# A window-attention block: the wide half of its second MLP matrix in three rounded passes

## The reference

```python
xn = layernorm(x, ln1_w, ln1_b)
xw = windows(jnp.roll(xn, (-3, -3), (1, 2)))          # (-1, 49, 192)
q, k, v = heads(xw @ qkv_w + qkv_b)
o = softmax(q @ k.T * 32 ** -0.5) @ v
x = x + unroll(o @ proj_w + proj_b)
h = layernorm(x, ln2_w, ln2_b)
h = gelu(h @ mlp_w1 + mlp_b1)                         # exact gelu, 768 wide
x = x + (h @ mlp_w2 + mlp_b2)
```

## Time and profile before

| | before |
|---|---|
| median of 3 runs | 3153.24 us (3152.94 to 3154.19) |
| profiled execution | 3154.41 us, its span 3152.6 us |
| TensorE matmuls | 3103.1 us, 98% of the span |
| TensorE weight loads | 2689.8 us, 85% |
| VectorE | 2200.5 us, 70% |
| ScalarE | 1971.1 us, 63% |
| GpSimd | 696.8 us, 22% |
| mean granted TensorE clock | 0.995 of full |

### The profile page before, as it was taken

How to read it: one execution, slowest core, us unless ns; L and a number is a source line. 1 busy time by engine, 2 the same in 40 slices (tenths; PEclk the granted TensorE clock), 3 DMA queues, 4 the chain that set the end, 5 groups by cost and what they waited for, 6 DMA issues and landing times.

```text
span 3152.6 us, 112135 instructions
## 1 busy us (share of the span) xinstructions
PE 3103.1 (98%) x44212; PEld 2689.8 (85%) x44212; DVE 2200.5 (70%) x5902; ACT 1971.1 (63%) x3595; POOL 696.8 (22%) x782
## 2 busy tenths in 40 slices
PE   6999999999999999999999999999999999999998
PEld 5888888888888888888888888888888888888887
DVE  4677777677776776677767777767776777767774
ACT  3666666666666666666666666666666666666664
POOL 1222222222222222222222222222222222222220
PEclk8999999999999999999999999999999999999999
DMA  1001001000100010001001000100010001001100
GB/s 45 25 26 28 23 23 28 26 23 23 29 25 23 25 28 23 23 26 28 23 23 27 26 23 23 29 25 23 23 29 24 23 25 28 23 23 26 27 23 17
DMA packets 112145, 79.77 MB, mean 25 GB/s; under 512 B 10129, under 2 KB 111603, under 8 KB 112115
## 3 DMA queue, kind: packets, MB, share of 16 engines
q1 hardware_dynamic: 112114, 79.35, 9.6%
HBM read 40.78 MB, written 38.54 MB: 25 GB/s over the span
## 4 chain that ended last, share of the span: by engine, by line
PE 97%; issue 1%; POOL 0%; DVE 0%; ACT 0%; DMA 0%; SPq 0%; POOLq 0%; DVEq 0%; ACTq 0%
PE ps L741 34%; PE ps L808 17%; PE ps L744 15%; PE ps L817 9%; PE ps L778 5%; PE ps L840 5%; PE ps L860 4%; PE ps L704 3%; PE ps L712 2%; PE ps L825 2%; PE ps L828 1%; PE ps L714 1%; DMA xin<-in_x 0%; POOL xb L355 0%; DVE st L391 0%
## 5 line engine op out<-in xcount | busy, mean ns | idle before, releaser
L741 PE MATMUL ps<-zh,w 128*128 128x392 f32 x3072 | 708.6, 345 | 0.6 <-ACT zh L586 0.6
L808 PE MATMUL ps<-g,w 128*128 128x392 f32 x1536 | 586.2, 504 | 0.0
L741 PEld LDWEIGHTS ps<-zh,w 128*128 128x128 f32 x3072 | 537.2, 189 | 22.3 <-ACT zh L586 0.9
L741 PE MATMUL ps<-zh,wqkv 128*128 128x400 f32 x1536 | 418.9, 381 | 0.0
L808 PEld LDWEIGHTS ps<-g,w 128*128 128x128 f32 x1536 | 261.2, 190 | 143.7 <-issue 36.5
L664 ACT ACTIVATE g<-ps,biasf 128x392 f32<-128x392 f32 x768 | 372.7, 563 | 3.3 <-PE ps L741 3.3
L363 POOL TENSOR_TENSOR ve<-mv,eps 98x4 f32<-98x4 f32 x256 | 50.9, 199 | 1402.2 <-DVE mv L396 1402.2
L391 DVE BATCH_NORM_STATS2 st<-xin 98x6 f32<-98x192 f32 x512 | 145.8, 348 | 302.8 <-DMA xin<-in_x 302.8
L629 ACT ACTIVATE yT<-ps,b 128x392 f32<-128x392 f32 x128 | 75.1, 587 | 422.5 <-PE ps L808 422.5
L404 DVE TENSOR_SCALAR z<-x,mv,rs 98x192 f32<-98x192 f32 (+2 forms) x768 | 208.5, 345 | 186.7 <-POOL rs L365 186.7
L741 PEld LDWEIGHTS ps<-zh,wqkv 128*128 128x128 f32 x1536 | 290.9, 190 | 41.6
(11 more groups left out here) (92 smaller groups left out, 5779.1 us busy)
## 6 DMA issues: line engine op xcount, KB each, us to landing
xin<-in_x SPq DMA_DIRECT2D x128, 147.0 KB
out<-yo SPq DMA_DIRECT2D x128, 147.0 KB
xin<-in_x SPq DMA_DIRECT2D x128, 71.2 KB
out<-yo SPq DMA_DIRECT2D x128, 71.2 KB
xin<-in_x SPq DMA_DIRECT2D x128, 54.8 KB
out<-yo SPq DMA_DIRECT2D x128, 54.8 KB
xin<-in_x SPq DMA_DIRECT2D x128, 18.8 KB
out<-yo SPq DMA_DIRECT2D x128, 18.8 KB
```

The source lines that it names most:

```text
L741: last = pe.matmul(dst, cols(w, part), act_ if zh is zh2 else windows(act_, WIDE, EVEN), start=(n == 0), stop=(n == 4))
L808: last = pe.matmul(ps[:, Y[0], 0:M], w2[:, k, 0:A], g[:, k, :], start=(k == 0), stop=(k == KC - 1))
```

## The change

The wide half of the second MLP matrix is computed in three rounded passes for each of its six chunks. The weight gets a high part `w2h` and a low part `w2l` once at the start. Of g, the high part `gh` is a copy that rounds, made for chunks 0 to 2 by ScalarE (`high_gelu`) and for 3 to 5 by GpSimd; the low part `gl` = g - gh is made by GpSimd for all six (`gelu_parts`), after its half of the normalisation and ahead of the two rstd computations. The narrow half stays float32. ScalarE does Gelus 0 to 3, roundings 0 and 1, the two copies of probabilities, rounding 2, Gelus 4 and 5. TensorE turns the probabilities before it transposes z1; the wide half stands as chunks 0 and 1 before pv, 2 and 3 after the narrow half, 4 and 5 after the projection, in each pair the low parts of g last. The banks move: q to 7, the result Y to 4 and 5, the probabilities to 4 then 2, the projection to 2 and 3. With them the waits move: pv waits for both copies, the projection for both low parts of its input before it starts, `turn_result` for the residual. TensorE waits for `projb_ready` before the first scores, as the bias product lies in bank 3. The copy of qA is in two parts (214 and 186 columns), and the second half of the scores of heads 0 to 3 waits for the second.

```diff
+        w2h = sb("w2h", [128, KC, A], F32R)
+        w2l = sb("w2l", [128, KC, A], F32R)
...
+        gh = sb("gh", [128, KC, M], F32R)
+        gl = sb("gl", [128, KC, M], F32R)
...
-        QK = (0, 1, 6)
+        QK = (7, 1, 6)
...
-        Y = (7, 6)
+        Y = (4, 5)
...
-        TP = (2, 4)
+        TP = (4, 2)
         PV = 2
-        PROJ = (4, 5)
+        PROJ = (2, 3)
         OFFSETS = (4, 7)
-        PROJ_OFFSET = 7
+        PROJ_OFFSET = 3
+        Q_CUT = 4 * EVEN + WIDE - EVEN
...
+        ACT_HIGH = 3
...
+            def gelu_parts(prev):
+
+                wait(pool, y_done, 2, prev - 1, 2)
+                for m in range(KC):
+                    if m < ACT_HIGH:
+                        wait(pool, gh_act, ACT_HIGH, prev, m + 1)
+                    else:
+                        wait(pool, g_done, KC, prev, m + 1)
+                        pool.nop(nofuse=True)
+                        pool.tensor_copy(gh[:, m, :], g[:, m, :]).then_inc(gh_pool, 1)
+                        wait(pool, gh_pool, KC - ACT_HIGH, prev, m + 1 - ACT_HIGH)
+                    pool.tensor_tensor(gl[:, m, :], g[:, m, :], gh[:, m, :].bitcast(F32), ALU.subtract)\
+                        .then_inc(gl_done, 1)
+
...
                     normalise(pool, i, 0)
+                if feeds(i):
+                    gelu_parts(i - 1)
+                if attends(i):
                     if more(i + 1):
                         rstd(mv1, ve1, rs1, mv1_done, ve1_done, rs1_done, i + 2, z1_done)
...
+                low_weight(W2, [(w2l[:, :, :], w2[:, :, 0:A], w2h[:, :, :], None)])
...
-                act.activation(qA[:, 0:N], ps[:, QK[0], 0:N], ACT.Identity, bias=biasf[:, Q0:Q0 + 1])\
-                   .then_inc(qk_ready, 1)
+                for cols in (slice(0, Q_CUT), slice(Q_CUT, N)):
+                    act.activation(qA[:, cols], ps[:, QK[0], cols], ACT.Identity, bias=biasf[:, Q0:Q0 + 1])\
+                       .then_inc(qk_ready, 1)
...
+            def high_gelu(prev, m):
+
+                wait(act, g_done, KC, prev, m + 1)
+                act.activation(gh[:, m, :], g[:, m, :], ACT.Copy).then_inc(gh_act, 1)
+
...
+                high_weight(W2, [(w2h[:, :, :], w2[:, :, 0:A], 1.0)])
...
-                    for m in range(KC):
-                        wait(act, h_done, KC, prev, m + 1)
-                        act.activation(g[:, m, :], ps[:, H[m], 0:M], ACT.Gelu, bias=biasf[:, HID0 + m:HID0 + m + 1])\
-                           .then_inc(g_done, 1)
+                    for m in range(4):
+                        gelu(prev, m)
+                    high_gelu(prev, 0)
+                    high_gelu(prev, 1)
...
+                if feeds(i):
+                    high_gelu(prev, 2)
+                    gelu(prev, 4)
+                    gelu(prev, 5)
                 if more(i):
                     wait(act, v_done, 1, i, 1)
                     high_parts1(i + 1)
...
-                wait(pe, qk_ready, 2, i, 2)
-                wait(pe, x2_done, 2, i - 1, 2)
+                wait(pe, qk_ready, 3, i, 2)
+                wait(pe, yT_ready, 2, i - 2, 2)
                 for q, k, heads, row, col in ((qA, kA, (0, 1, 2, 3), 0, 0), (qB, kB, (4, 5), 64, PAIRS * TOK)):
                     for half in range(2):
+                        if half == 1 and q is qA:
+                            wait(pe, qk_ready, 3, i, 3)
...
+                dst = ps[:, Y[0], 0:M]
+                if 0 in chunks and attends(prev + 1):
+                    wait(pe, pt_ready, 2, prev + 1, 1)
                 for k in chunks:
-                    wait(pe, g_done, KC, prev, max(k + 1, H.index(Y[0]) + 1))
-                    last = pe.matmul(ps[:, Y[0], 0:M], w2[:, k, 0:A], g[:, k, :], start=(k == 0), stop=(k == KC - 1))
+                    if k < ACT_HIGH:
+                        wait(pe, gh_act, ACT_HIGH, prev, k + 1)
+                    else:
+                        wait(pe, gh_pool, KC - ACT_HIGH, prev, k + 1 - ACT_HIGH)
+                    pe.matmul(dst, w2h[:, k, :], gh[:, k, :], start=(k == 0), stop=False)
+                    pe.matmul(dst, w2l[:, k, :], gh[:, k, :], start=False, stop=False)
+                for k in chunks:
+                    wait(pe, gl_done, KC, prev, k + 1)
+                    last = pe.matmul(dst, w2h[:, k, :], gl[:, k, :], start=False, stop=(k == KC - 1))
...
+                if attends(prev + 1):
+                    wait(pe, x2_done, 2, prev + 1, 2)
...
-                    if feeds(i) and half == 0:
-                        wait(pe, g_done, KC, i - 1, 4)
+                    if feeds(i):
+                        wait(pe, g_done, KC, i - 1, 2 * half + 2)
...
+                wait(pe, pt_ready, 2, i, 2)
+                pe.nop(nofuse=True)
                 for half in range(2):
-                    wait(pe, pt_ready, 2, i, half + 1)
-                    pe.nop(nofuse=True)
...
-                wait(pe, oh_ready, 2, i, 1)
+                wait(pe, ol_ready, 2, i, 2)
                 for p in range(BLOCKS):
-                    waits = {} if p else {2: [(ol_ready, 2, i, 1)], 3: [(ol_ready, 2, i, 2)]}
...
             pe.wait_ge(pads_ready, 2)
+            pe.wait_ge(projb_ready, 1)
...
+                if attends(i):
+                    turn_probs(i)
                 if more(i):
                     wait(pe, z1_done, 1, i + 1, 1)
                     wait(pe, s_sub, 2, i, 2)
                     transposes1()
-                if attends(i):
-                    turn_probs(i)
-                if feeds(i):
-                    mlp2_wide(prev, range(0, 3))
+                if feeds(i):
+                    mlp2_wide(prev, (0, 1))
                 if attends(i):
                     pv(i)
                 if feeds(i):
                     mlp2_narrow(prev)
-                    mlp2_wide(prev, range(3, 4))
+                    mlp2_wide(prev, (2, 3))
                 if attends(i):
                     proj(i)
                 if feeds(i):
-                    mlp2_wide(prev, range(4, KC))
+                    mlp2_wide(prev, (4, 5))
```

More of the change, by code:

```diff
@@ L164, in swin_kernel @@
         g_done = sem("g_done")
+        gh_act = sem("gh_act")
+        gh_pool = sem("gh_pool")
+        gl_done = sem("gl_done")
         y_done = sem("y_done")
@@ L613, in values, with gelu @@
                                ACT.Copy).then_inc(v_ready, 1)
+            def gelu(prev, m):
+                wait(act, h_done, KC, prev, m + 1)
+                act.activation(g[:, m, :], ps[:, H[m], 0:M], ACT.Gelu, bias=biasf[:, HID0 + m:HID0 + m + 1])\
+                   .then_inc(g_done, 1)
+            def high_gelu(prev, m):
+                wait(act, g_done, KC, prev, m + 1)
+                act.activation(gh[:, m, :], g[:, m, :], ACT.Copy).then_inc(gh_act, 1)
             def exponential(i, part, slots):
@@ L750, in qk @@
                 wait(pe, zl1_done, 2, i, 2)
-                if tiles == (2,):
-                    wait(pe, yT_ready, 2, i - 2, 1)
                 for t in tiles:
@@ L867, in proj @@
                     pe.wait_ge(w_lo, PROJ_W + 1)
-                wait(pe, oh_ready, 2, i, 1)
+                wait(pe, ol_ready, 2, i, 2)
                 for p in range(BLOCKS):
-                    waits = {} if p else {2: [(ol_ready, 2, i, 1)], 3: [(ol_ready, 2, i, 2)]}
                     last = project(ps[0:PART, PROJ[p // 2], 256 * (p % 2):256 * (p % 2) + C], oh, ol, wproj,
-                                   lambda w, part: w[:, part, :], tokens=span(p), waits=waits)
+                                   lambda w, part: w[:, part, :], tokens=span(p))
                     if p % 2:
@@ L904, in body @@
                         pe.wait_ge(weight_loaded[W2], 16 * LOADS[W2])
-                        pe.wait_ge(w_lo, W1 + 1)
+                        pe.wait_ge(w_lo, W2 + 1)
                     mlp1(prev)
@@ L909, in body @@
                     pe.wait_ge(consts_loaded, 16 * NCONST)
-                    pe.wait_ge(projb_ready, 1)
                     offsets(1, raw_w1, [(HID0 + k, 0, 128 * k, 128) for k in range(KC)])
                     pe.wait_ge(bias_ready, 2)
+                if attends(i):
+                    turn_probs(i)
                 if more(i):
```

## The result

The changed kernel takes 3095.99 us (median of 4 runs, 3093.59 to 3099.09) where the kernel before takes 3153.62 on the same chips: 0.982 of the time, 95% interval 0.980 to 0.983. The forecast was 3080 in a range of 3038 to 3125, faster with a chance of 0.86. Direction and range held; the time is 16 us above the forecast, and the loop that sets the group is one that the forecast had as not quite the last.

A forecast was written before the change was run, and what follows sets the result against it. TensorE nearly alone bounded the 24.14 us group; less work there would leave two loops at 23.5. 127 groups gave -81, edges +6.7 and +1: 3154.4 - 74 = 3080 us, range 3038 to 3125.

The forecast's parts named there:

- The passes: TensorE, wide half: eighteen rounded passes at 0.178 us for twelve float32 at 0.332, saving 0.70 us a group.
- q's copy: ScalarE's copy before the scores, in two parts: scores start earlier, saving TensorE 0.2 to 0.25 us a group.
- two loops: Once-per-group loops through VectorE and through the input load: both 23.5 us, longer than TensorE's 23.2.
- The waits that take over: TensorE waits before the probabilities' second half and before the projection, replacing saved time: a group 23.5 us.
- The loop that the forecast summed: Second residual, result, VectorE's normalisation, then TensorE back to the residual: 6.22 + 8.43 + 8.83 = 23.5 us.
- the input loop: Result's stores, next load, VectorE's statistics, low parts, projection, result: 11.06 + 4.05 + 0.1 + 2.1 + 6.22 = 23.5 us.
- GpSimd: Its subtractions (0.9 us) and copies (0.5), 7.2 us a group, stay beside TensorE's work with cover 2.5.
- Rival 3: GpSimd's nine operations at 1.19 us each become the bound: a group 24.7, 3233 us, slower; chance 0.10.
- The edges: Start: bias wait, weight rounding, z1 transposes, +6.7 us; end: last group's bare GpSimd chain, +1 us.
- The wait for the bias: Start: first scores and values wait for the projection bias, so they precede the bias matmuls: 5.2 us.
- The sum: Whole kernel: 127 groups give -81 us, edges +6.7 and +1, together -74, so 3080 us.

The follow-up runs named there:

- float32 run: Changed kernel's order, banks and q copy, with the wide half back in float32 and no rounded or low part of g: 3176.64 us, a group 24.26.
- when GpSimd's is short: Changed kernel with GpSimd's half of the probabilities' normalisation cut to 1 of 12 slots, the rest left unnormalised: 3064.23 us, a group 23.36.
- the mended kernels: Changed kernel with z1's scaling behind the normalisation and projection bias in bank 7, 3062.64 us; then one low pass of g moved later, 3054.32 us.
- three extra subtractions: Changed kernel with three more unused 128x392 GpSimd subtractions a group ahead of the last low part: 3254.33 us, a group 24.80.
- both mends: Changed kernel with z1's scaling moved behind VectorE's half of the normalisation and the projection's bias product back in bank 7: 3062.64 us, a group 23.36.

## Why the prediction was right or wrong

**The passes: right.** Forecast -0.70 us a group, measured -0.66 (the float32 run against the changed kernel; the other 0.04 is the wait for the probabilities, 0.26 there and 0.30 here). In the trace of the changed kernel the rounded passes of the wide half stand 0.18 apart, by their starts in one third, against the 0.332 of the earlier trace rows:

```profile
1503.21 0.34 PE L859 MATMUL ps<-gh,w2l 128*128 128x392 f32 x1
...
1503.40 0.34 PE L858 MATMUL ps<-gh,w2h 128*128 128x392 f32 x1
...
1503.57 0.34 PE L859 MATMUL ps<-gh,w2l 128*128 128x392 f32 x1
```

**q's copy: right for TensorE, nearly nothing for the kernel.** The copy's first part ends 0.2 earlier, and undoing it costs 0.03 a group, as two loops that don't contain it said it would.

**The waits that take over: right in size, wrong in place.** The forecast was 23.5 a group by two loops; it is 23.58, and 23.60 with the odd groups. That the turned order of the transposes puts a wait before the probabilities was right. But the working took GpSimd's half as just in time (9.30 against 9.31) and VectorE's as late. It is the other way round: GpSimd's ends at 1520.04 - 1510.60 = 9.44 into the group, where TensorE wants it at 9.38, and TensorE takes it up 0.27 later; I had put 0.07 for that. VectorE's half ends at 1519.69 + 0.97 = 1520.66, while its first transpose, the seventh of twelve, starts at 1520.94. The loop that the forecast summed therefore lies at most 0.3 under the one that binds: that its 23.5 came so near is in part luck, as the two halves end close together and the input loop, which gave the same 23.5, was mis-sized. VectorE's multiplication, when GpSimd's is short, takes 0.77, so it is held up by 0.20 and not by 0.35; the part of its 0.97 that lies behind the end of GpSimd's isn't its whole free time. Summed by its rows, the loop is 6.25 (second residual to result's end), 6.42 (to the end of the first reciprocal), 1.27 (GpSimd), 0.27, and 9.39 from the first transpose to the next second residual at 1529.70: 23.60.

The Trainium skill, "SBUF — State Buffer", section "Who interferes with whom", has a VectorE instruction with two SBUF inputs and a GpSimd instruction that reads SBUF shut each other out. That holds in kind: VectorE's multiplication took 0.97 beside GpSimd's, 0.77 clear of it.

**The input loop: mis-sized.** Forecast 23.5, in truth 23.25: the statistics start 10.79 and 10.99 after the result's end in two groups shown by

```profile
1487.74 1.01 DVE L536 TENSOR_TENSOR yo<-ps,x 98x512 f32<-98x512 f32 x2
...
1499.54 1.14 DVE L417 BATCH_NORM_STATS2 st<-xin 98x6 f32<-98x192 f32 x4 [2.46 <-DMA xin<-in_x]
...
1523.34 1.14 DVE L417 BATCH_NORM_STATS2 st<-xin 98x6 f32<-98x192 f32 x4 [2.67 <-DMA xin<-in_x]
```

mean 10.89 and not 11.06, and the projection takes 2.0 to the second residual and not 2.1. 10.89 + 4.01 + 0.1 + 2.0 + 6.25 = 23.25, which is 0.33 under the group. It became the bound only in the mended kernels.

**GpSimd: right that it is covered, its price low by a tenth.** A subtraction takes 1.02 and costs 0.97 to 0.99 by its starts, where 0.9 stood; a copy 0.51, as put. The cover was 1.8 and not 2.5. The Trainium skill's 2.6 cycles for an element ("GPSIMD Engine Reference", section 3.1) had given 0.85; the measured 1.02 is 0.17 above it, about the fixed part of a small instruction (0.20 for four columns, above). Rival 3 was a fair rival: at 1.13 for each of the nine it would have decided; three extra subtractions did.

**The edges: the start right in cause, the end not foreseen.** Start +7.5 against +6.7. The wait for the bias, which I had put at 5.2, is 7.1 in one pair of profiled executions and 2.3 in the other, 5.1 and 4.1 by the medians; the scores and values behind it took 6.0. End +4.4 against +1. From the last group's z2 transposes (3072.25) to its last low pass (3088.17 + 0.44) are 16.4 us, 16.1 before, but that hides two differences. From the start of the wide half to its end are 8.1 us (from 3080.53), 6.5 before (3137.27 to 3143.77): +1.6 for GpSimd's chain, where +1 was forecast. The MLP ahead of it, from those transposes to the wide half, took 1.3 less, with the granted clock at 0.65 and then 0.98 where before it was 0.50 and then 0.88. Nearly all the rest is a pause of TensorE in the next to last body, for which no releaser shows, and the slow narrow half behind it:

```profile
3059.83 0.32 PE L916 MATMUL ps<-pt,vt 49*32 49x49 f32 x2 [2.46 <-issue]
3060.08 3.71 PE L871 MATMUL ps<-g,w 128*64 128x196 f32 x24
```

The narrow half takes 3.71 at a granted clock of 0.57 (3060.0 to 3063.7), 2.21 in a steady group, so pause and clock together are 4.0 us. The same pause, 1.9 to 2.5 us, stands in seven of the twelve kernels of the experiments and is missing in the five others and in the kernel before; with the bias in bank 7 alone it is missing, with both mends it is there. Those with it need 51.9 us or more behind the last start of the scores, those without 48.9 to 50.3. A like pause of 1.4 us stands in the group of 25.3 near the start. What TensorE waits for there stays open; it wasn't tried, and one profiled execution of each kernel can't say whether the pause belongs to the kernel or to the execution. It may have to do with the wider spread of the changed kernel's runs, 5.5 us against 1.3, but that is only argued.

**The sum.** -81 for the groups was -67 (126 groups by 0.54 and not 0.64), +7.7 at the edges was +11.9. The 14 us in the groups are the step that missed most: 0.08 a group in the loop's size, 10 us, and 0.02 in the two or three odd groups, 3. The profiled execution (3099.1 us) is itself 3 above the median.

## What to carry to other kernels

When an engine is full and gets less to do, sum each loop that closes once per iteration, through every engine, and rank them: here four lay within 0.4 us of one another in a group of 23.6, and each mend moved the bound to the next. A product moved forward in an engine's order must be set against both of its sources, and the source nearest to just in time is the one to look at, with its wake-up in the sum. The dearest slack was elsewhere: moving one VectorE operation with some 3.5 us to spare behind one with none brought 29 us, half as much as the whole change.

## What of the hardware was not expected

TensorE starts 0.27 us after GpSimd's multiplication of 588 columns ends by the profile (0.24 on average), where VectorE follows GpSimd's last small operation by 0.1 (1508.68 + 1.01 to 1509.79). It isn't a late signal. The records of TensorE's own queue in that gap are two:

```profile
L182 PEldq EVENT_SEMAPHORE  x1: 51/51/51, 1520.1 to 1520.1; - x1
L182 PEldq FUSED_REGOPS  x1: 37/37/37, 1520.2 to 1520.2; - x1
```

In each of eighty steady groups the semaphore record starts 0.04 us after GpSimd's end and the register operation some 0.15 after it; the first transpose follows at 0.24. By the code a second wait, for a Gelu long done, stands between the wait for GpSimd and the first transpose, and this register operation is most likely its. In the run with three more subtractions only one wait stands before the low pass, and TensorE starts 0.06 after GpSimd's end (1503.95 + 1.00 to 1505.01). Putting the wait that ends last in the last place might therefore save more than 0.1 us a group; that wasn't tried.
